# GpSimd makes the f32 normalised rows of tiles 1 to 3, and the sum of V's squares stands four products sooner in TensorE's list

## The chip, the cores and the metric

The kernel runs on one core of a Trainium2 chip. The metric is the device time of one execution in microseconds (us), the median of several runs. The engines are named as the profile names them: PE is TensorE's matmul unit, DVE is VectorE, ACT is ScalarE, POOL is GpSimd, SP is SyncE, whose queue issues most DMAs.

## The reference

Two gated blocks follow each other on x, which is 2 batches of 1024 rows of 2048 numbers in f32:

```
q(v, s, z) = (clip(round(v / s + z), 0, 255) - z) * s
x1 = x  + tanh(g_xattn) * ( q(layernorm(x)) @ q(ctx) )        # ctx: one 2048 x 2048 matrix per batch
y  = x1 + tanh(g_ffn)   * ( layernorm(x1) @ (U * S @ V.T).T ) # U, V: 2048 x 512, S: 512
```

The second product is computed in two steps with rank 512: h = layernorm(x1) @ V, then h @ (U * S).T.

## The kernel before

The 2048 rows are 16 tiles of 128 rows (8 per batch); a tile's row block is split in four column units of 512, and for some steps in two halves of 1024. Each engine has its own instruction list, written out by hand, and the engines meet through semaphores.

For a tile t the steps are these. `s1` is the quantised product on PE (64 matmuls, 16 for each column unit). POOL's `pre_row` and `pre` prepare the residual row in `ring`, with one multiplication over the row and four additions of the column correction. DVE's `x1_unit` adds the product to it (L1137) and takes its statistics (L1139). `stats2` makes mean and scale of the second layernorm (L1150 to L1162). Then the normalised row is written as a high and a low f16 part: ACT writes the high part of a half (`x_hi_half`, L811), DVE writes the normalised half in f32 into `xn` (L1174) and then the low part as the difference of `xn` and the high part (L1177); both lines stand in `x_lo_half`. `xn` is one buffer of one half, 128x1024. SP transposes the half by DMA into `xT` (L339), and PE's `mm3` multiplies it with the high and low parts of V, 24 matmuls for each half (L584, L589). `mm4` is the product with U (L650, L651, L655).

V and U are scaled by a power of two taken from their norms. ACT squares V in eight pieces (L859); PE sums these squares across the partitions with a product with ones (`norm_sums(0)`, L668); DVE's `norm_sum_up(0)` and `norm(0)` make the scale of it. Then ACT writes V's high parts (L877) and DVE its low parts (`v_low`, L1246) in eight pieces, between the low parts of tiles 0 and 1. PE's first product with V (tile 0, `mm3(0)`) takes the low parts in the order in which they are made. U follows in the same way (`u_low`, L1252).

On DVE the order around the change is: the last three `x1_unit` of tiles 0 to 2 with `norm(0)` between them, `x_lo` of tile 0, one unit of tile 3, `v_low` 0 and 1 with the statistics of tile 1 between, `v_low` 2 and 3, `x_lo_half(1, 0)`, `v_low` 4 to 7, `x_lo_half(1, 1)`, the statistics of tile 2, `norm(1)`, `hid_lo(0)`, `u_low(0)`, `x_lo` of tile 2, `u_low` 1 and 2, one unit of the output, `u_low(3)`. `x_lo` of tile 3 comes some 15 us later.

Of the kernel before, what the change touches and what calls it, by code (L numbers as in the profile page):

```python
# [7 lines left out]
def gated_block_program(nc, x, ctx_in, params, U_t, S, V, out):  # L8
    f32, bf16, f16 = mybir.dt.float32, mybir.dt.bfloat16, mybir.dt.float16
    i32, u8 = mybir.dt.int32, mybir.dt.uint8  # L10
    ALU, ACT, AX = mybir.AluOpType, mybir.ActivationFunctionType, mybir.AxisListType
# [8 lines left out]
    NQ = D // W  # L20
# [6 lines left out]
    G = 3  # L27
# [2 lines left out]
    GW = P // CG  # L30
    H_PE = (5, 6, 7)
    X_PE = TB - 1
    NU8 = 8
    EPS = 1e-5
    MAGIC = 1.5 * 2.0 ** 23
# [11 lines left out]
    with es:  # L47
# [3 lines left out]
        def sem(name):  # L51
            return es.enter_context(nc.semaphore(name))
# [8 lines left out]
        xn = sb("xn", [P, HW], f32)  # L61
# [3 lines left out]
        stage = sb("stage", [P, 2, CK, W], f32)  # L65
        u8r = sb("u8r", [P, NU8, CK * W], u8)
        ident_b = sb("ident_b", [P, P], bf16)
# [8 lines left out]
        ln2 = sb("ln2", [P, 2, 10], f32)  # L76
# [77 lines left out]
        ln2_ready = sem("ln2_ready")  # L154
# [8 lines left out]
        x1_ready = sem("x1_ready")  # L163
        st2_ready = sem("st2_ready")
        xn_ready = sem("xn_ready")
        xs_hi = sem("xs_hi")
        xs_lo = sem("xs_lo")
        mm3_half = sem("mm3_half")
# [26 lines left out]
        h_bank = lambda u: bank[3 + u % 2]  # L195
        x_dma = lambda u: u + 1 - (u > X_PE)
        x_bank = lambda g, half: bank[(2 * g + half) % 3]
# [12 lines left out]
        xhalf = lambda t, g: ring[:, t % R, (1 - g) * HW:(2 - g) * HW]  # L210
# [26 lines left out]
        @block.gpsimd  # L237
        def _(pool):
            def op2(c):
                b, n, i = chunk(c)  # L240
                if c in POOL_WHOLE:
                    pool.wait_ge(SPOT[c][1], LANDED[c])
                    nc.gpsimd.tensor_scalar(u8r[:, c % NU8, :], flat2(SPOT[c][0]), C_R2, P_Z2, ALU.mult, ALU.add)\  # L243
                        .then_inc(ctx_u8_pool, 1)
                    pool.wait_ge(ctx_u8_pool, POOL_WHOLE.index(c) + 1)
                else:
                    pool.wait_ge(ctx_u8, act_u8(c))
                if c == 0:
                    pool.wait_ge(centre_ready, 1)
                if b > 0:  # L250
                    pool.wait_ge(s1_done, unit(TB * b - 1, n) + 1)
                nc.gpsimd.tensor_scalar(q2_chunk(c), u8r[:, c % NU8, :], C_NC2, 1.0, ALU.add, ALU.mult)\  # L252
                    .then_inc(q2_pool, 1)

            def pre_row(t):
                pool.wait_ge(q_u8, part_count(t))
                pool.wait_ge(row_ready, t + 1)
                nc.gpsimd.tensor_scalar(xt(t), xt(t), bvec[:, t % R, 1:2], 1.0, ALU.add, ALU.mult).then_inc(x1_row, 1)  # L258

            def pre(t, n):  # L260
                pool.wait_ge(x1_row, t + 1)
                pool.wait_ge(corr_ready, NQ * (t // TB) + n + 1)
                nc.gpsimd.tensor_tensor(xq(t, n), xq(t, n), corr[:, n * W:(n + 1) * W], ALU.add).then_inc(x1_pre, 1)  # L263

            nc.gpsimd.memset(ident_b[:, :], 0.0).then_inc(setup_ready, 1)
            nc.gpsimd.memset(ones_f[:, :], 1.0).then_inc(setup_ready, 1)
            nc.gpsimd.memset(ones_b[:, :], 1.0).then_inc(setup_ready, 1)
            nc.gpsimd.memset(C_EPS, EPS).then_inc(setup_ready, 1)
            pool.wait_ge(setup_ready, 4)
            nc.gpsimd.affine_select(out=ident_b[:, :], in_=ident_b[:, :], compare_op=ALU.not_equal, fill=1.0,  # L270
                                    base=0, pattern=[[-1, P]], channel_multiplier=1).then_inc(ident_ready, 1)
            nc.gpsimd.memset(ones_h[:, :], 4.0 / GW).then_inc(setup_ready, 1)

            for c in range(CQ):
                if not on_dve(c):
                    op2(c)
            for n in range(NQ - 1):
                for i, c in enumerate(range(CQ * (n + 1), CQ * (n + 2), 2)):
                    op2(c)
                    if n == 0 and i < G:  # L280
                        pre_row(i)
                for t in range(G):
                    pre(t, n)
            for t in range(G):
                pre(t, NQ - 1)
            for t in range(G, NT):
                if t == TB:
                    for c in range(CB, 2 * CB):
                        op2(c)
                if t == G:  # L290
                    pool.wait_ge(t_written, 2 * G)
                    nc.gpsimd.memset(ident_h, 0.0).then_inc(ident_free, 1)
                    pool.wait_ge(ident_free, 1)
                    nc.gpsimd.affine_select(out=ident_h, in_=ident_h, compare_op=ALU.not_equal, fill=1.0, base=0,
                                            pattern=[[-1, P]], channel_multiplier=1).then_inc(ident_ready, 1)
                if t not in (6, 7):
                    pre_row(t)
                    for n in range(NQ):
                        pre(t, n)
                elif t == 6:  # L300
                    for v, n in MIXED:
                        if n == 0:
                            pre_row(v)
                        pre(v, n)
# [181 lines left out]
        def _(pe):  # L486
# [46 lines left out]
            def s1_part(t, n, k0=0, k1=KT):  # L533
                i = unit(t, n)
                if k0 == 0:
                    if t < G:
                        if n == 0:
                            pe.wait_ge(t_read, 2 * t + 1)
                        if n >= 2:
                            pe.wait_ge(x1_ready, unit(t, n - 2) + 1)  # L540
                    else:
                        if n == 0:
                            pe.wait_ge(qT_in, 16 * (t - G + 1))
                        if i < NQ * G + 3:
                            pe.wait_ge(x1_ready, unit(i - NQ * G, 2) + 1)
                        else:
                            pe.wait_ge(x1_ready, i - 2)
                        if t == TB and n == 0:
                            pe.wait_ge(corr_ready, 2 * NQ - 1)
                for k in range(k0, k1):  # L550
                    if t < G and n == 0 and k == KT // 2:
                        pe.wait_ge(t_read, 2 * t + 2)
                    mm = nc.tensor.matmul(unit_bank(t, n)[:, :], qT_of(t)[:, k, :], q2[:, n, k, :],  # L553
                                          start=(k == 0), stop=(k == KT - 1))
                if k1 == KT:
                    mm.then_inc(s1_done, 1)
# [5 lines left out]
            def mm3(u):  # L562
# [12 lines left out]
                for g in range(2):  # L575
                    if u == X_PE:
                        pe.wait_ge(xT_copied, 2 * g + 2)
# [15 lines left out]
            def x_pieces(g):  # L593
                pe.wait_ge(xs_hi, 2 * X_PE + g + 1)
                pe.wait_ge(xs_lo, 2 * X_PE + g + 1)
                for half in range(2):
# [99 lines left out]
                    for t in range(G if n < NQ - 1 else 1):  # L696
                        s1_part(t, n, CK * i, CK * i + CK)
            s1_part(1, NQ - 1)
            s1_part(2, NQ - 1, 0, 12)
            norm_sums(0)  # L700
            s1_part(2, NQ - 1, 12)
            s1(G)
            mm3(0)
            norm_sums(1)
# [43 lines left out]
        def _(act):  # L748
            def op1(c):
                act.wait_ge(SPOT[c][1], LANDED[c])  # L750
                if c >= NU8 and c < CB or c >= CB + NU8:
                    if on_dve(c - NU8):
                        act.wait_ge(q2_dve, dve_count(c - NU8))
# [50 lines left out]
            def x_hi_half(u, g):  # L804
                scale, bias = ln2[:, u % 2, 8:9], ln2[:, u % 2, 9:10]
                act.wait_ge(ln2_ready, u + 1)
                if u - 1 == X_PE:
                    act.wait_ge(xT_written, 2 * g + 2)
# [228 lines left out]
        def _(dve):  # L1037
            ts, stt, tt = nc.vector.tensor_scalar, nc.vector.scalar_tensor_tensor, nc.vector.tensor_tensor
# [129 lines left out]
            def x_lo_half(u, g):  # L1168
                mean, scale = ln2[:, u % 2, 0:1], ln2[:, u % 2, 8:9]
                if 2 * u + g > 0:  # L1170
                    dve.wait_ge(xs_lo, 2 * u + g)
                if u == 6 and g == 0:
                    dve.wait_ge(ctx_u8, act_u8(XN_CHUNK))
                ts(xn[:, :], xhalf(u, g), mean, scale, ALU.subtract, ALU.mult).then_inc(xn_ready, 1)  # L1174
                dve.wait_ge(xn_ready, 2 * u + g + 1)
                dve.wait_ge(xs_hi, 2 * u + g + 1)
                tt(xs[:, g, 1, :], xn[:, :], xs[:, g, 0, :], ALU.subtract).then_inc(xs_lo, 1)  # L1177

# [4 lines left out]
            def xT_copy(g):  # L1183
                for half in range(2):
                    dve.wait_ge(xT_written, 2 * g + half + 1)
                    dve.wait_ge(mm3_half, 2 * (X_PE - 1) + g + 1)
                    nc.vector.tensor_copy(xT[:, g, half, :, :].rearrange("p k w -> p (k w)"),
# [280 lines left out]
```

## Time and profile before

| | |
|---|---|
| median of 3 runs | 604.24 us (603.97 to 604.48) |
| the profiled execution | 604.71 us, its span 602.9 us |
| PE busy | 582.7 us, 97% of the span |
| DVE busy | 381.7 us, 63% |
| ACT busy | 212.4 us, 35% |
| POOL busy | 191.4 us, 32% |
| granted clock of TensorE | 1.000 |

All times of an event are microseconds from the start of the span. PE's matmuls overlap each other in the records: one of 512 columns is shown with 0.38 us, and begins 0.216 us behind the one before it. The name in front of the arrow is the tile that an instruction writes, those behind it are what it reads; `bank` is PSUM, the others are SBUF. The low part of V reads V from the space that is later `u_hl`, and so stands as `v_hl<-u_hl,wsc,v_hl`.

### The profile page before, as it was taken

To read this page: it belongs to the slowest core of one execution; us is meant where nothing else is said; L and a number is where in the kernel's file an instruction comes from. 1 tells how busy PE (TensorE), PEld (TensorE's weight loads), DVE (VectorE), ACT (ScalarE), POOL (GpSimd) and SP (SyncE) were. 2 spreads that over 40 slices of the span, in tenths; PEclk is the share of its full clock that TensorE was granted. 3 is DMA by queue.
4 is the path that set the end of the run, shared out by engine and by line. 5 is a ranking of instruction groups with operands and counts; after the bars stand their busy time and mean duration, and the time that the engine had idled before them with its cause. 6 is when DMAs were issued, how large, how long until landed. Compare 5 with 4: busy or idle time off the path is not lost.

```text
span 602.9 us, 7571 instructions
## 1 busy us (share of the span) xinstructions
PE 582.7 (97%) x2816; PEld 266.4 (44%) x2816; DVE 381.7 (63%) x703; ACT 212.4 (35%) x258; POOL 191.4 (32%) x149
## 2 busy tenths in 40 slices
PE   1899999999999999999999999999999999999998
PEld 1344444444444444445444444444444444444444
DVE  6939989995288962845375975647365665735212
ACT  5798978822041432456623310303011030301000
POOL 2899650002223419726505800220404030030000
DMA  8999985639828795998835344370906345181512
GB/s 280 387 387 387 309 240 128 116 122 196 239 55 240 186 216 189 241 304 268 241 123 150 81 84 54 66 190 12 223 35 147 116 90 172 30 163 20 138 53 104
DMA packets 143828, 102.21 MB, mean 170 GB/s; under 512 B 106672, under 2 KB 106928, under 8 KB 143792
## 3 DMA queue, kind: packets, MB, share of 16 engines
q1 hardware_dynamic: 134800, 84.43, 53.1%
q10 hardware_dynamic: 8992, 17.30, 9.2%
q8 instruction: 22, 0.36, 0.2%
q14 instruction: 14, 0.11, 0.1%
HBM read 58.99 MB, written 16.78 MB: 126 GB/s over the span
## 4 chain that ended last, share of the span: by engine, by line
PE 75%; DMA 11%; DVE 8%; issue 3%; SPq 2%; ACT 1%; POOL 1%; DVEq 0%; ACTq 0%
PE bank L553 23%; PE bank L584 16%; PE bank L651 8%; PE bank L650 8%; PE bank L655 8%; PE bank L589 8%; DMA v_hl<-in_ctx_dram 8%; DMA xT<-xs 4%; DVE v_hl L1246 1%; DVE xn L1174 1%; DVE xs L1177 1%; DVE ring L1137 1%; SPq L311 1%; PE bank L520 1%; POOL u8r L243 1%
## 5 line engine op out<-in xcount | busy, mean ns | idle before, releaser
L553 PE MATMUL bank<-q,qT 128*128 128x512 bf16 x896 | 201.5, 380 | 0.3 <-DVE ring L1137 0.3
L553 PEld LDWEIGHTS bank<-q,qT 128*128 128x128 bf16 x896 | 87.7, 98 | 107.1 <-issue 1.5
L258 POOL TENSOR_SCALAR ring<-ring,bvec 128x2048 f32<-128x2048 f32 x16 | 32.8, 2050 | 269.7 <-DVE bvec L1119 269.7
L584 PE MATMUL bank<-v_hl,xT 128*128 128x512 f16 x512 | 115.8, 379 | 0.9 <-DMA xT<-xs 0.9
L263 POOL TENSOR_TENSOR ring<-ring,corr 128x512 f32<-128x512 f32 x64 | 87.0, 1390 | 23.2 <-ACT corr L850 22.1
L651 PE MATMUL bank<-u_hl,hbuf 128*128 128x512 f16 x240 | 91.1, 380 | 0.0
L650 PE MATMUL bank<-u_hl,hbuf 128*128 128x512 f16 x240 | 91.0, 379 | 0.0
L1137 DVE SCALAR_TENSOR_TENSOR ring<-bank,const,ring 128x512 f32<-128x512 f32 x64 | 47.6, 743 | 58.2 <-PE bank L553 55.9
L1210 DVE SCALAR_TENSOR_TENSOR ring<-bank,cy,ring 128x512 f32<-128x512 f32 x63 | 46.4, 747 | 52.8 <-PE bank L655 52.8
L252 POOL TENSOR_SCALAR q<-u8r,const 128x1024 bf16<-128x1024 uint8 x52 | 63.9, 1236 | 45.4 <-ACT u8r L756 41.7
L584 PEld LDWEIGHTS bank<-v_hl,xT 128*128 128x128 f16 x512 | 49.8, 98 | 61.2 <-DMA xT<-xs 1.9
L797 ACT ACTIVATE ln<-ln,const 128x1 f32<-128x1 f32 x16 | 4.7, 294 | 189.8 <-DVE ln L1150 189.8
L655 PE MATMUL bank<-u_hl,hbuf 128*128 128x512 f16 x240 | 61.6, 379 | 0.0
L589 PE MATMUL bank<-v_hl,xT 128*128 128x512 f16 x256 | 60.6, 379 | 0.0
L1177 DVE TENSOR_TENSOR xs<-xn,xs 128x1024 f16<-128x1024 f32 x32 | 46.8, 1461 | 9.7 <-ACT xs L811 8.8
L1078 DVE BATCH_NORM_STATS2 st<-ring 128x6 f32<-128x512 f32 x64 | 40.3, 680 | 10.3 <-DMA ring<-in_x_dram 10.2
L1139 DVE BATCH_NORM_STATS2 st<-ring 128x6 f32<-128x512 f32 x64 | 44.5, 695 | 2.2
L811 ACT ACTIVATE xs<-ring,ln 128x1024 f16<-128x1024 f32 x32 | 38.2, 1233 | 20.4 <-DVE ln L1162 14.8
L589 PEld LDWEIGHTS bank<-v_hl,xT 128*128 128x128 f16 x256 | 25.0, 98 | 30.4 <-DVE v_hl L1246 0.4
L650 PEld LDWEIGHTS bank<-u_hl,hbuf 128*128 128x128 f16 x240 | 23.5, 98 | 28.5 <-issue 0.4
L655 PEld LDWEIGHTS bank<-u_hl,hbuf 128*128 128x128 f16 x240 | 23.5, 98 | 28.3
L1193 DVE SCALAR_TENSOR_TENSOR hbuf<-bank,hbuf 128x512 f16<-128x512 f32 x16 | 11.0, 687 | 39.4 <-ACT hbuf L825 39.4
(136 smaller groups left out, 493.3 us busy)
## 6 DMA issues: line engine op xcount, KB each, us to landing
out_dram<-ring SPq DMA_DIRECT2D x63, 256.0 KB, 3.5
ring<-in_x_dram SPq DMA_DIRECT2D x62, 256.0 KB, 3.9
v_hl<-in_ctx_dram SPq DMA_DIRECT2D x26, 512.0 KB, 11.5
stage<-in_ctx_dram ACTq DMA_DIRECT2D x17, 512.0 KB, 5.8
u_hl<-in_L_ffn_V_dram SPq DMA_DIRECT2D x8, 512.0 KB, 11.5
corr<-in_ctx_dram ACTq DMA_DIRECT2D x8, 512.0 KB, 6.7
stage<-in_ctx_dram SPq DMA_DIRECT2D x6, 512.0 KB, 11.5
q<-in_ctx_dram ACTq DMA_DIRECT2D x4, 512.0 KB, 8.8
```

What stands on the lines that cost most here:

```text
L252: nc.gpsimd.tensor_scalar(q2_chunk(c), u8r[:, c % NU8, :], C_NC2, 1.0, ALU.add, ALU.mult)\
L263: nc.gpsimd.tensor_tensor(xq(t, n), xq(t, n), corr[:, n * W:(n + 1) * W], ALU.add).then_inc(x1_pre, 1)
L553: mm = nc.tensor.matmul(unit_bank(t, n)[:, :], qT_of(t)[:, k, :], q2[:, n, k, :], start=(k == 0), stop=(k == KT - 1))
L584: nc.tensor.matmul(h_bank(u)[:, :], xT[:, g, half, k % 8, :], v_hl[:, k, 0, :], start=(g == 0 and a == 0 and half == 0), stop=False)
L589: mm = nc.tensor.matmul(h_bank(u)[:, :], xT[:, g, 0, k % 8, :], v_hl[:, k, 1, :], start=False, stop=(g == 1 and a == 7))
L650: nc.tensor.matmul(y_bank(i)[:, :], t_hi[:, r, :], u_hl[:, n, r, 0, :], start=(r == 0), stop=False)
L651: nc.tensor.matmul(y_bank(i)[:, :], t_lo[:, r, :], u_hl[:, n, r, 0, :], start=False, stop=False)
L655: mm = nc.tensor.matmul(y_bank(i)[:, :], t_hi[:, r, :], u_hl[:, n, r, 1, :], start=False, stop=(r == RT - 1))
L1137: stt(xq(t, n), unit_bank(t, n)[:, :], C_A, xq(t, n), ALU.mult, ALU.add).then_inc(x1_ready, 1)
L1139: nc.vector.bn_stats(st2[:, t % R, n, :], xq(t, n)).then_inc(st2_ready, 1)
L1177: tt(xs[:, g, 1, :], xn[:, :], xs[:, g, 0, :], ALU.subtract).then_inc(xs_lo, 1)
L1210: stt(xq(u, n), y_bank(i)[:, :], cy[:, n:n + 1], xq(u, n), ALU.mult, ALU.add).then_inc(y_ready, 1)
```

## The change

POOL gets six new instructions behind the four additions of tile 3: for tiles 1, 2 and 3 and both halves it writes `xn`. Each waits for the tile's mean and scale (`ln2_ready`) and for the difference before it (`xs_lo`), since `xn` is one buffer. DVE leaves out its own six and waits for POOL's (`xn_pool`). Besides, PE's `norm_sums(0)` moves from behind the twelfth to behind the eighth of the sixteen products of tile 2's last unit.

```diff
+    XN_POOL = (1, 2, 3)
...
+        xn_pool = sem("xn_pool")
...
+            def normalised_x(u, g):
+                mean, scale = ln2[:, u % 2, 0:1], ln2[:, u % 2, 8:9]
+                pool.wait_ge(ln2_ready, u + 1)
+                pool.wait_ge(xs_lo, 2 * u + g)
+                nc.gpsimd.tensor_scalar(xn[:, :], xhalf(u, g), mean, scale, ALU.subtract, ALU.mult).then_inc(xn_pool, 1)
...
                     pre_row(t)
                     for n in range(NQ):
                         pre(t, n)
+                    if t == G:
+                        for u in XN_POOL:
+                            for g in range(2):
+                                normalised_x(u, g)
...
             s1_part(1, NQ - 1)
-            s1_part(2, NQ - 1, 0, 12)
+            s1_part(2, NQ - 1, 0, 8)
             norm_sums(0)
-            s1_part(2, NQ - 1, 12)
+            s1_part(2, NQ - 1, 8)
...
-                ts(xn[:, :], xhalf(u, g), mean, scale, ALU.subtract, ALU.mult).then_inc(xn_ready, 1)
-                dve.wait_ge(xn_ready, 2 * u + g + 1)
+                if u in XN_POOL:
+                    dve.wait_ge(xn_pool, 2 * XN_POOL.index(u) + g + 1)
+                else:
+                    ts(xn[:, :], xhalf(u, g), mean, scale, ALU.subtract, ALU.mult).then_inc(xn_ready, 1)
+                    dve.wait_ge(xn_ready, 2 * (u - sum(v < u for v in XN_POOL)) + g + 1)
                 dve.wait_ge(xs_hi, 2 * u + g + 1)
                 tt(xs[:, g, 1, :], xn[:, :], xs[:, g, 0, :], ALU.subtract).then_inc(xs_lo, 1)
```

The lists of the engines, first POOL's, before, from the identity matrix to tile 5's additions:

```order
L292 MEMSET ident_b 128x128
L294 AFFINE_SELECT ident_b<-ident_b 128x128
L258 TENSOR_SCALAR ring<-ring,bvec 128x2048
L263 TENSOR_TENSOR ring<-ring,corr 128x512 x4
L258 TENSOR_SCALAR ring<-ring,bvec 128x2048
L263 TENSOR_TENSOR ring<-ring,corr 128x512 x4
```

and POOL's of the change, at the same place:

```order
L300 MEMSET ident_b 128x128
L302 AFFINE_SELECT ident_b<-ident_b 128x128
L260 TENSOR_SCALAR ring<-ring,bvec 128x2048
L271 TENSOR_TENSOR ring<-ring,corr 128x512 x4
L266 TENSOR_SCALAR xn<-ring,ln 128x1024 x6
L260 TENSOR_SCALAR ring<-ring,bvec 128x2048
```

The six new instructions stand between tile 3's additions and tile 4's row.

DVE's list before, from the last scale of tile 1 to its second difference and the first statistics of tile 2 (`v_hl<-` is a low part of V):

```order
L1162 TENSOR_SCALAR ln<-ln 128x1
L1246 SCALAR_TENSOR_TENSOR v_hl<-u_hl,wsc,v_hl 128x2x512 x2
L1174 TENSOR_SCALAR xn<-ring,ln 128x1024
L1177 TENSOR_TENSOR xs<-xn,xs 128x1024
L1246 SCALAR_TENSOR_TENSOR v_hl<-u_hl,wsc,v_hl 128x2x512 x4
L1174 TENSOR_SCALAR xn<-ring,ln 128x1024
L1177 TENSOR_TENSOR xs<-xn,xs 128x1024
L1150 BN_AGGR ln<-st 128x2
```

and DVE's of the change:

```order
L1174 TENSOR_SCALAR ln<-ln 128x1
L1261 SCALAR_TENSOR_TENSOR v_hl<-u_hl,wsc,v_hl 128x2x512 x2
L1192 TENSOR_TENSOR xs<-xn,xs 128x1024
L1261 SCALAR_TENSOR_TENSOR v_hl<-u_hl,wsc,v_hl 128x2x512 x4
L1192 TENSOR_TENSOR xs<-xn,xs 128x1024
L1162 BN_AGGR ln<-st 128x2
```

The differences are left (now L1192), and the two that made `xn` are gone from between the low parts of V.

PE's list before, around the sum of V's squares (`bank<-ssq,ones_f`):

```order
L516 MATMUL bank<-q,ones_b 128x512 x2
L553 MATMUL bank<-q,qT 128x512 x2
L553 MATMUL bank<-q,xT 128x512 x28
L668 MATMUL bank<-ssq,ones_f 128x8
L553 MATMUL bank<-q,xT 128x512 x4
L553 MATMUL bank<-q,qT 128x512 x64
```

and PE's of the change:

```order
L528 MATMUL bank<-q,ones_b 128x512 x2
L565 MATMUL bank<-q,qT 128x512 x2
L565 MATMUL bank<-q,xT 128x512 x24
L680 MATMUL bank<-ssq,ones_f 128x8
L565 MATMUL bank<-q,xT 128x512 x8
L565 MATMUL bank<-q,qT 128x512 x64
```

Four of the products that stood ahead of the sum now stand behind it.

## Rows read from the trace of the kernel before

**Rows 1.** The page's first part: busy us, share of the span, instructions.

```profile
PE 582.7 (97%) x2816; PEld 266.4 (44%) x2816; DVE 381.7 (63%) x703; ACT 212.4 (35%) x258; POOL 191.4 (32%) x149
```

**Rows 2.** PE's waits: us in total, times, longest.

```profile
PE bank L516 <- POOL q L252: 13.6, 4, 11.3
...
PE bank L584 <- DMA xT<-xs: 0.9, 2, 0.5
```

**Rows 3.** PE's timeline, 76 to 109 us: start, us, instruction, [idle before, releaser].

```profile
76.95 0.28 PE L668 MATMUL bank<-ssq,ones_f 128*128 128x8 f32 x2
...
100.40 1.99 PE L589 MATMUL bank<-v_hl,xT 128*128 128x512 f16 x8
102.22 0.29 PE L668 MATMUL bank<-ssq,ones_f 128*128 128x8 f32 x2
...
105.81 1.89 PE L589 MATMUL bank<-v_hl,xT 128*128 128x512 f16 x8
108.12 3.63 PE L584 MATMUL bank<-v_hl,xT 128*128 128x512 f16 x16 [0.41 <-DMA xT<-xs]
```

**Rows 4.** The chain that ended last, 98 to 108 us: start, us, what.

```profile
98.05 3.67 DVE v_hl L1246 x3
...
102.49 1.24 DVE xs L1177
...
103.80 4.27 DMA xT<-xs
```

**Rows 5.** DVE's timeline, 77 to 103 us.

```profile
77.28 0.17 DVE L1223 TENSOR_REDUCE wsc<-bank 128x1 f32<-128x8 f32 x1 [1.22 <-PE bank L668]
...
82.27 0.85 DVE L1174 TENSOR_SCALAR xn<-ring,ln 128x1024 f32<-128x1024 f32 x1
83.15 2.18 DVE L1177 TENSOR_TENSOR xs<-xn,xs 128x1024 f16<-128x1024 f32 x1
...
92.49 2.47 DVE L1246 SCALAR_TENSOR_TENSOR v_hl<-u_hl,wsc,v_hl 128x1024 f16<-128x1024 f32 x2
94.88 0.81 DVE L1174 TENSOR_SCALAR xn<-ring,ln 128x1024 f32<-128x1024 f32 x1
95.72 1.23 DVE L1177 TENSOR_TENSOR xs<-xn,xs 128x1024 f16<-128x1024 f32 x1
96.86 4.87 DVE L1246 SCALAR_TENSOR_TENSOR v_hl<-u_hl,wsc,v_hl 128x1024 f16<-128x1024 f32 x4
```

**Rows 6.** ACT's timeline, the last square of V.

```profile
74.08 0.19 ACT L859 ACTIVATION_READ_ACCUMULATOR hbuf<-u_hl 128x1 f32 x1
```

**Rows 7.** Timelines of POOL and of DVE where both work.

```profile
81.28 2.96 POOL L263 TENSOR_TENSOR ring<-ring,corr 128x512 f32<-128x512 f32 x2
...
207.01 2.11 POOL L263 TENSOR_TENSOR ring<-ring,corr 128x512 f32<-128x512 f32 x1
...
208.03 1.64 DVE L1174 TENSOR_SCALAR xn<-ring,ln 128x1024 f32<-128x1024 f32 x1
209.71 2.17 DVE L1177 TENSOR_TENSOR xs<-xn,xs 128x1024 f16<-128x1024 f32 x1
```

**Rows 8.** Single lines: ns min/median/max, first and last start, forms.

```profile
L1177 DVE TENSOR_TENSOR xs<-xn,xs x32: 1224/1226/2873, 83.2 to 554.9; 128x1024 f16<-128x1024 f32 x32
...
L1137 DVE SCALAR_TENSOR_TENSOR ring<-bank,const,ring x64: 730/745/753, 44.6 to 548.2; 128x512 f32<-128x512 f32 x64
...
L258 POOL TENSOR_SCALAR ring<-ring,bvec x16: 1965/1972/2399, 32.4 to 526.4; 128x2048 f32<-128x2048 f32 x16
...
L243 POOL TENSOR_SCALAR u8r<-v_hl,const,par x5: 1188/1190/1618, 13.6 to 23.9; 128x1024 uint8<-128x1024 f32 x5
...
L263 POOL TENSOR_TENSOR ring<-ring,corr x64: 1259/1268/2249, 43.3 to 532.1; 128x512 f32<-128x512 f32 x64
```

**Rows 9.** Timelines of DVE and of PE, tile 2 and the last low parts of U.

```profile
113.36 1.23 DVE L1177 TENSOR_TENSOR xs<-xn,xs 128x1024 f16<-128x1024 f32 x1
...
120.47 2.73 DVE L1252 SCALAR_TENSOR_TENSOR u_hl<-u8r,us_scale,u_hl 128x512 f16<-128x512 f32 x4
...
122.80 1.03 PE L655 MATMUL bank<-u_hl,hbuf 128*128 128x512 f16 x4
```

## The prediction

> **What bounds the kernel now.** The page's first part comes first: TensorE (PE) is busy for 582.7 of the 602.9 us of the span [rows 1]. The view of PE's waits then says what the rest is: 13.6 us behind POOL's quantised chunks, in the opening stage, and of the small ones the one that lies at this change is for a DMA of xs into xT, 0.9 us in two waits [rows 2]. So a change around tiles 1 to 3 can only give back what PE loses there, and everything else it does matters only if it makes PE wait anew.
>
> What PE loses there is read from its timeline. A product with 512 columns is shown with 0.38 us, and 16 of them with 3.63 [rows 3], so each follows the one before in (3.63 - 0.38) / 15, about 0.216 us. The second half of tile 1's product with V should follow eight products that begin at 105.81, that is at 105.81 + 8 x 0.216 = 107.54; it begins at 108.12 [rows 3]: 0.58 us lost. Eight products from 100.40 should hand over at 102.13, and the next begins at 102.22: 0.09 lost. The sum is 0.67 us, and this is the most that the change can save here.
>
> The chain that ended last says who is late at both places [rows 4]. VectorE (DVE) ends the last low part of V at 101.73 (98.05 + 3.67), then makes xn, then the difference xs until 103.72; the transposing DMA of tile 1's second half lands 4.27 us after 103.80, and PE starts. So DVE's list from 77 to 104 us is the term to be costed. In it the reader should see one thing: DVE is busy without a gap from 77.28 to 103.72, with xn (0.81 us each), the differences (1.23 us) and the eight low parts (2.47 us for two, 4.87 for four) [rows 5].
>
> **Part 1, the sum of squares four products sooner.** The last square ends at 74.27 (74.08 + 0.19) [rows 6]; the sum would now stand at 76.95 - 4 x 0.216 = 76.09, still 1.8 us behind it, so PE has nothing to wait for. PE's own work is the same. DVE, which took this sum at 77.28, takes it at 76.42: 0.86 us earlier. How far does this get? xn of tile 0 began at 82.27 [rows 5] and would begin at 81.41. But POOL is adding the correction to row 3: one addition starts at 81.28 and two of them last 2.96 us, until 84.24 [rows 7]. Group 7 also shows what happens when these two engines meet: at 208.03 xn takes 1.64 us instead of 0.81, and at 209.71 the difference takes 2.17 instead of 1.23, beside an addition that takes 2.11 us instead of 1.27 [rows 7, 8]. They take turns: each instruction waits for the other engine's to end. In the profile shown the difference at 83.15 took 2.18 us [rows 5], so it ended 1.1 us behind POOL's additions, which is nearly its own whole length. With xn at 81.41, POOL's third addition is already in (it began 0.13 us before), xn ends near 83.1 as now, the fourth addition comes next, and the difference still ends at 85.33. The 0.86 us end there. I cost part 1 at nothing; if DVE were to come in ahead, that is a rival below.
>
> **Part 2, POOL makes xn of tiles 1 to 3.** Removed from DVE: six instructions of 0.81 us, with 0.03 us to the next start: 0.84 each (94.88 to 95.72) [rows 5]. Added on POOL: six tensor_scalar of 128x1024 in f32, which no row shows. From below: half of POOL's 128x2048 one, 1.97 / 2 = 0.99 us; from above, of this kind, the one of 128x1024 that writes uint8, 1.19 us [rows 8]. I take 1.1, between them. POOL's timeline is empty from 84.24 until row 4's correction, behind tile 3's differences, so nothing of POOL's list is queued behind the new waits that anyone needs; it issues no DMA here either.
>
> What the cover costs is DVE's. For tile 1 POOL can begin when the scale is ready, near 92.6, and DVE is then in two low parts of V that began at 92.49, with four more from 96.86 in front of the second half [rows 5]. Such a low part reads two tensors in SBUF (V in f32 and its high part). No row shows this instruction beside a working POOL. The nearest rows are the differences, which also read two tensors in SBUF and are stretched (1.22 us at least, up to 2.87), while L1137, which reads one from PSUM and one from SBUF, never goes above 0.753 us in 64 [rows 8]. I therefore take it that the low parts take turns with POOL as the differences do. The stretch is 2.17 - 1.23 = 0.94 us behind an addition of 1.27 us, and 0.94 - (1.27 - 1.10) = 0.77 behind one of 1.1 us. I take 0.85, between these. The bounds are 0 (no turns at all) and 1.27 (one whole addition).
>
> The Trainium skill (SBUF — State Buffer, Who interferes with whom) says that a VectorE instruction with two SBUF inputs contends with a GpSimd instruction that reads SBUF, and that whichever issues first holds the shared ports for its whole length while the other fully blocks. The differences' rows agree with it, and it speaks against this change: by it the work moved to POOL still takes VectorE's time at the low parts.
>
> The sum for tile 1. First half: DVE saves 0.84 and loses 0.85 at the low part behind POOL. Second half: POOL's instruction falls among the four low parts, and these are late by the first half's 0.01 plus 0.85. The last low part ends at 101.73 + 0.86 = 102.59. PE needs it for the last two of its eight products from 100.40, and had it just in time; so PE is now 0.86 us late and would reach tile 1's second half at 107.54 + 0.86 = 108.40. The second difference gets its own 0.84 back and ends at 103.74, against 103.72; the DMA lands near 108.1, before PE is there. The stall of 0.58 us is gone and a new one of 0.86 + the old 0.09 has taken its place, one stage earlier: PE goes on at 108.40 instead of 108.12, **0.28 us later**.
>
> Tile 2: its two differences follow each other on DVE, and xn is a single buffer, so the second xn can only start behind the first difference. DVE saves 0.84 once and then stands for POOL's 1.1 us and two semaphores instead of its own 0.84: about 0.5 us saved at best, and the first difference has to wait for ScalarE's half anyway. The two end near 114.6, as now (113.36 + 1.23) [rows 9]. What is behind them is the low parts of U, the last of which run from 120.47 to 123.20, while PE takes the first of them at 122.80 and one every 0.22 us, the fourth at 123.45 [rows 9]: 0.25 us to spare, 0.5 with PE 0.28 late. I cost it at nothing; without the cover it costs what DVE is later by. Tile 3 saves DVE about 0.5 us too, where it waits for PE soon after: nothing.
>
> After 125 us the rows of PE's waits name only fractions of a microsecond, and DVE, ACT and the DMA queues follow PE's progress, so 0.28 us is carried to the end. Against the profiled execution, 604.71 (span 602.9 and 1.8 around it), this makes 605.0; its own time lies 0.47 above the median of the runs, 604.24, and on that median it makes **604.5**.
>
> **Rivals.** (a) The low parts don't take turns with POOL. For it: no row shows them together. Against: the differences do. Then the last low part ends at 100.0, the difference near 102.1, and PE has neither stall: 604.24 - 0.67 = 603.6. Chance 0.14.
> (b) The 0.86 us of part 1 get through, because DVE comes in before POOL's third addition. For it: only 0.13 us decide. Against: the fourth addition still has to be passed. Then the last low part is where it was, 101.73, the DMA lands at 107.2 and PE runs on at 107.54: 603.7. Chance 0.10.
> (c) The slower side: POOL's new instruction holds the turn longer. The mechanism is the one of the sum, its price is PE's lateness of 2h - 0.84 - 0.58, with h the stretch of one low part. It passes 1.2 us from h = 1.31. For it: POOL's additions cost 1.27 us for 512 columns, and at that rate 1024 columns would be 2.5 us, with h near 2.2 and PE 3.0 us late: 607.2. Against: its tensor_scalar rows, with one tensor read, run at under 1 ns a column. At the upper bound of h, 1.27, it makes 604.24 + 1.12 = 605.4. Chance of more than 1.2 us: 0.08.
> (d) The low parts, issued back to back, keep POOL out until the list has a gap. Then DVE stands for POOL's 1.1 us at each half: the second difference ends about 0.7 later and so does the DMA, near 108.8: 604.9. It has the forecast's sign and is counted with it.
>
> **The numbers.** The forecast with (d) has 0.62, with a range of its own of 604.3 to 604.9. The rivals (a) to (c) have 0.14, 0.10 and 0.08, and 0.06 is for what I have not seen, such as a transfer that falls elsewhere. The range goes from (a) less the spread of the runs (0.2) to (c) at its upper bound plus the same: 603.4 to 605.6. A measurement of this kernel tells about 0.2%, 1.2 us, from no change. Faster than 603.0 needs (a) and part of another stall too: 0.05. Slower than 605.4: (c) and a share of the unseen, 0.10. Within: 0.85.
>
> **What the changed profile would show.** Right: the low parts of V beside POOL's xn last about 2.1 us instead of 1.3, one in each half of tile 1; PE stops for about 0.9 us before 102 to 103 us, behind the low part of V, and no longer behind the DMA of xs; the first difference of tile 0 still ends near 85.3. Wrong: low parts that keep 1.3 us with POOL working (a), tile 0's difference near 84.5 (b), POOL's xn above 1.3 us (c), POOL starting only when the low parts are through (d), or a PE wait beyond 125 us that is new and longer than half a microsecond.

## The result and the profile after

The change makes the kernel slower: 612.94 us median of 4 runs (612.34 to 613.82) against 604.36 of before beside it, a ratio of 1.0143 (95% interval 1.013 to 1.0156). The forecast was 604.5 with a range of 603.4 to 605.6. The profiled execution has a span of 610.5 us, 7.6 more than before.

The page's first part of the changed kernel, which answers to [rows 1] (some matmul records are missing):

```profile
PE 585.1 (96%) x2787; PEld 267.1 (44%) x2816; DVE 379.7 (62%) x697; ACT 212.4 (35%) x258; POOL 218.0 (36%) x155
```

DVE has lost six instructions, but POOL has gained 26.6 us for six. The view of one line says why; it is POOL's new instruction, ns min/median/max:

```profile
L266 POOL TENSOR_SCALAR xn<-ring,ln x6: 3782/3784/5854, 92.3 to 141.8; 128x1024 f32<-128x1024 f32 x6
```

It takes **3.78 us** where nothing disturbs it. The prediction had 1.1, between 0.99 and 1.19. Its timeline, POOL, 90 to 146 us:

```profile
92.34 5.85 POOL L266 TENSOR_SCALAR xn<-ring,ln 128x1024 f32<-128x1024 f32 x1 [8.43 <-DVE ln L1174]
99.68 5.71 POOL L266 TENSOR_SCALAR xn<-ring,ln 128x1024 f32<-128x1024 f32 x1 [1.49 <-DVE xs L1192]
...
115.77 3.78 POOL L266 TENSOR_SCALAR xn<-ring,ln 128x1024 f32<-128x1024 f32 x1 [3.61 <-DVE xs L1192]
```

And DVE's timeline at the same place, which answers to [rows 5]:

```profile
92.14 2.47 DVE L1261 SCALAR_TENSOR_TENSOR v_hl<-u_hl,wsc,v_hl 128x1024 f16<-128x1024 f32 x2
98.28 1.22 DVE L1192 TENSOR_TENSOR xs<-xn,xs 128x1024 f16<-128x1024 f32 x1 [3.67 <-POOL xn L266]
99.42 5.65 DVE L1261 SCALAR_TENSOR_TENSOR v_hl<-u_hl,wsc,v_hl 128x1024 f16<-128x1024 f32 x4
...
119.64 1.23 DVE L1192 TENSOR_TENSOR xs<-xn,xs 128x1024 f16<-128x1024 f32 x1 [4.05 <-POOL xn L266]
```

The two low parts from 92.14 keep their length (2.47), and it is POOL that waits: 5.85 us is 3.78 and 2.07 more. Then DVE stands for 3.67 us. From 92.14 to the end of the last low part at 105.07 it takes 12.93 us, against 9.24 before (92.49 to 101.73). In front of the second half it is one of the four low parts that is held up as well, the third, with 2.05 us instead of 1.28:

```profile
101.83 2.05 DVE L1261 SCALAR_TENSOR_TENSOR v_hl<-u_hl,wsc,v_hl 128x1024 f16<-128x1024 f32 x1
```

PE's timeline pays for it, beside [rows 3]:

```profile
100.76 0.61 PE L601 MATMUL bank<-v_hl,xT 128*128 128x512 f16 x2 [0.40 <-DVE v_hl L1261]
101.96 0.60 PE L601 MATMUL bank<-v_hl,xT 128*128 128x512 f16 x2 [0.60 <-DVE v_hl L1261]
103.94 0.60 PE L601 MATMUL bank<-v_hl,xT 128*128 128x512 f16 x2 [1.37 <-DVE v_hl L1261]
105.13 1.03 PE L601 MATMUL bank<-v_hl,xT 128*128 128x512 f16 x2 [0.59 <-DVE v_hl L1261]
...
106.25 6.14 PE L596 MATMUL bank<-v_hl,xT 128*128 128x512 f16 x16
```

Each pair of products stands for its low part of V, 3.0 us in all. The sixteen products from 106.25 take 6.14 us instead of 3.6: the windows view has a mean granted clock of 0.56 from 105.90 to 112.20, so PE ran there mostly at 1.2 of its 2.4 GHz (columns: us, busy by engine, clock, DMA share, GB/s):

```profile
105.90:112.20 6.30, 6.30 (x19) 2.48 (x18) 5.85 (x22) 2.53 (x6) 3.78 (x1) 0.56 0.44 85
```

From 105.13 to the products at 112.22 PE takes 7.09 us; the same work takes 4.04 in experiment 5 (106.01 to 110.05), where the granted clock is 1.0. PE begins the product with U at 119.13 instead of 113.31, and 3.05 of these 5.82 us are the slower clock. A second loss comes at tile 5, where PE waits for qT, the tile's transposed quantised row. From PE's timeline:

```profile
187.44 13.76 PE L565 MATMUL bank<-q,qT 128*128 128x512 bf16 x62 [1.88 <-DMA qT<-qn]
```

This product began at 178.92 before, without a wait: PE is 8.5 us late here. The chain that ended last leads from the slow instruction at tile 3, through DVE and the output's DMAs, to tile 5's transposition (us from start, us, what):

```profile
136.54 3.79 POOL xn L266
...
145.68 1.23 DVE xs L1192
...
182.91 4.26 DMA qT<-qn
```

Behind it some small waits of before are gone, such as the one for xs that ended at 268.99, and the span ends 7.6 us later.

### The profile page after: what moved, and what is told of

It is laid out like the page before. It is cut to its first block, busy times and chain, and to the rows that moved or that the text cites. A ratio compares the mean times of both kernels' runs of the same rounds, so it can differ in the third digit from the quotient of the medians.

```text
span 610.5 us, 7548 instructions
## 1 busy us (share of the span) xinstructions
PE 585.1 (96%) x2787; PEld 267.1 (44%) x2816; DVE 379.7 (62%) x697; ACT 212.4 (35%) x258; POOL 218.0 (36%) x155
## 4 chain that ended last, share of the span: by engine, by line
PE 66%; DVE 10%; DMA 9%; POOL 6%; issue 3%; ACT 3%; SPq 2%; ACTq 0%; DVEq 0%; POOLq 0%
PE bank L565 22%; PE bank L596 14%; PE bank L662 7%; PE bank L667 7%; PE bank L663 7%; PE bank L601 7%; POOL xn L266 3%; DMA stage<-in_ctx_dram 2%; DVE xs L1192 2%; DMA u_hl<-in_L_ffn_V_dram 2%; DMA v_hl<-in_ctx_dram 2%; DMA out_dram<-ring 2%; POOL ring L271 1%; DVE u_hl L1267 1%; DVE ring L1149 1%
## 5 line engine op out<-in xcount | busy, mean ns | idle before, releaser
L565 PE MATMUL bank<-q,qT 128*128 128x512 bf16 x873 | 198.6, 380 | 3.5 <-DMA qT<-qn 1.9
L596 PE MATMUL bank<-v_hl,xT 128*128 128x512 f16 x512 | 118.2, 385 | 0.0
L601 PE MATMUL bank<-v_hl,xT 128*128 128x512 f16 x256 | 61.4, 381 | 3.0 <-DVE v_hl L1261 3.0
L1192 DVE TENSOR_TENSOR xs<-xn,xs 128x1024 f16<-128x1024 f32 x32 | 46.8, 1461 | 23.1 <-POOL xn L266 14.4
L266 POOL TENSOR_SCALAR xn<-ring,ln 128x1024 f32<-128x1024 f32 x6 | 26.7, 4450 | 35.0 <-DVE ln L1174 28.4
```

The costliest lines, as they stand in the source:

```text
L266: nc.gpsimd.tensor_scalar(xn[:, :], xhalf(u, g), mean, scale, ALU.subtract, ALU.mult).then_inc(xn_pool, 1)
L596: nc.tensor.matmul(h_bank(u)[:, :], xT[:, g, half, k % 8, :], v_hl[:, k, 0, :], start=(g == 0 and a == 0 and half == 0), stop=False)
L601: mm = nc.tensor.matmul(h_bank(u)[:, :], xT[:, g, 0, k % 8, :], v_hl[:, k, 1, :], start=False, stop=(g == 1 and a == 7))
```

## The experiments

Intervals are those of the ratio to the kernel before, run on the same chip.

**1. The same change with another operation.** ALU.add with -mean, which `ln2` holds already, in place of ALU.subtract with the mean.

```diff
-                mean, scale = ln2[:, u % 2, 0:1], ln2[:, u % 2, 8:9]
+                neg, scale = ln2[:, u % 2, 2:3], ln2[:, u % 2, 8:9]
-... xhalf(u, g), mean, scale, ALU.subtract, ALU.mult)
+... xhalf(u, g), neg, scale, ALU.add, ALU.mult)
```

Expected: 

> The changed kernel with one operation replaced: GpSimd makes xn as (x + neg) * scale, with neg = -mean, which VectorE has written already, instead of (x - mean) * scale. Theory (the subtraction is what makes GpSimd's instruction take 3.78 us): it takes 1.0 to 1.2 us; the low parts of V wait little, TensorE's four waits before 106 us shrink to under 1 us, its clock stays at 1.0, and the time is 604.0 to 605.2 us. Rival (two column scalars with an f32 output are slow whatever the operation): the instruction stays at 3.8 us and the time at 612 to 614 us.

Measured: 605.15 us, ratio 1.0014 (1.0006 to 1.0023). The line of the new instruction, DVE's stretched low part and PE's waits in this kernel:

```profile
L266 POOL TENSOR_SCALAR xn<-ring,ln x6: 1195/1196/3273, 92.7 to 133.9; 128x1024 f32<-128x1024 f32 x6
```

```profile
99.56 2.05 DVE L1261 SCALAR_TENSOR_TENSOR v_hl<-u_hl,wsc,v_hl 128x1024 f16<-128x1024 f32 x1
```

```profile
PE bank L565 <- DMA qT<-qn: 1.0, 1, 1.0
PE bank L601 <- DVE v_hl L1261: 0.8, 2, 0.6
```

One operation takes 3.78 us down to 1.20 and about nine tenths of the loss away. The 1.0 us at qT is a single wait before 180.80, at tile 5, where the kernel before had none.

**2. Which forms are slow.** Eight instructions at an idle end of POOL's list, in the kernel before.

```diff
+            for s1_, s2_, o1, o2 in forms:
+                pool.wait_ge(probe, done)
...
+                    ins = nc.gpsimd.tensor_scalar(pb, pa, s1_, s2_, o1, o2)
+                ins.then_inc(probe, 1)
```

Expected: 

> The kernel before, with two fills and eight GpSimd tensor_scalar instructions of 128x1024, f32 to f32, in an idle end of GpSimd's list behind tile 15's last difference, each waiting for the one before; they compute nothing that is used. In order: (subtract, mult), (add, mult), (mult, add), all three with two columns; (subtract, mult) and (add, mult) with a column and the constant 1.0; (mult, subtract) with two columns; subtract alone; add alone. Theory (subtraction is slow): 3.8 us for the forms with subtract, 1.0 to 1.2 us for those with add and mult. Rival (two columns are slow): the first, second, third and sixth take 3.8 us, the others near 1.1. The kernel's time is that of before, since nothing waits for them.

Measured: POOL's timeline, in the order of the list:

```profile
556.78 3.79 POOL L325 TENSOR_SCALAR stage<-stage,pc 128x1024 f32<-128x1024 f32 x1
560.67 1.19 POOL L325 TENSOR_SCALAR stage<-stage,pc 128x1024 f32<-128x1024 f32 x1
561.96 1.19 POOL L325 TENSOR_SCALAR stage<-stage,pc 128x1024 f32<-128x1024 f32 x1
563.25 3.70 POOL L325 TENSOR_SCALAR stage<-stage,pc 128x1024 f32<-128x1024 f32 x1
567.05 1.11 POOL L325 TENSOR_SCALAR stage<-stage,pc 128x1024 f32<-128x1024 f32 x1
568.27 3.78 POOL L325 TENSOR_SCALAR stage<-stage,pc 128x1024 f32<-128x1024 f32 x1
572.14 2.86 POOL L323 TENSOR_SCALAR stage<-stage,pc 128x1024 f32<-128x1024 f32 x1
575.09 2.85 POOL L323 TENSOR_SCALAR stage<-stage,pc 128x1024 f32<-128x1024 f32 x1
```

Every pair with subtract takes 3.70 to 3.79 us, (add, mult) and (mult, add) 1.11 to 1.19, with two columns or one. Each form ran once. The rival falls, and so does one part of the theory: subtract alone takes 2.86 us where 3.8 were expected, and add alone takes 2.85, as long. So it is the pair (add, mult) or (mult, add) that is fast, not the addition. Why the pairs differ, no run shows. The kernel took 604.25 us.

**3. The sum's new place alone.** Expected: 

> The kernel before with only the sum of V's squares moved four products ahead; VectorE makes every xn. Theory (the turn-taking with GpSimd's additions at 81 to 84 us eats what VectorE gains): tile 0's first difference ends within 0.4 us of where it did, 85.3, and the time is that of before within 0.5 us. Rival (the gain gets through to the last low part of V): up to 0.7 us less than before.

The edit is the last part of the change without the rest. Measured: 604.37 us, ratio 1.0003 (0.9995 to 1.0012). DVE's timeline in this kernel:

```profile
81.43 1.70 DVE L1174 TENSOR_SCALAR xn<-ring,ln 128x1024 f32<-128x1024 f32 x1
83.17 2.18 DVE L1177 TENSOR_TENSOR xs<-xn,xs 128x1024 f16<-128x1024 f32 x1
```

xn begins 0.84 us sooner than in [rows 5] and takes 0.85 longer. Nothing gets through.

**4. GpSimd's part alone.** The change with `norm_sums(0)` behind the twelfth product. Expected: 

> The changed kernel with the sum of V's squares at its old place; GpSimd makes xn of tiles 1 to 3 with the subtraction. Theory (all of the loss is the six instructions of 3.78 us): 612 to 614 us, as the whole change. Rival (the sum's new place has a share of the loss): below 611 us.

Measured: 614.72 us, ratio 1.0173 (1.0157 to 1.0189). The whole loss and 0.3% more, a little above the 612 to 614 us expected. In this execution POOL's second instruction took 6.90 us instead of 5.71: it was let in one low part later, so one run of the turns costs a low part more than the other. That this is all of the 0.3% isn't shown.

**5 and 6. Which tile.** XN_POOL = (1,) and XN_POOL = (2, 3), both with the subtraction. Expected of the first: 

> The changed kernel with GpSimd making xn of tile 1 only, still with the subtraction; VectorE makes that of tiles 2 and 3. Theory (the loss is made at tile 1, where the low parts of V wait in line behind the first difference): TensorE starts the first product with U about 5.8 us later than before, as in the whole change, and the time is 610 to 613.5 us. Rival (tiles 2 and 3 make most of it): under 608 us.

Of the second: 

> The changed kernel with GpSimd making xn of tiles 2 and 3 only, with the subtraction. VectorE's second difference of tile 2 then ends about 3 us later than before (3.8 us of GpSimd in place of 0.84 of its own), and behind it the low parts of U had 0.25 us to spare. Theory (each tile's pair has its own cover, tile 2's is 0.25 us): TensorE waits 2 to 3 us for the low parts of U, 606 to 608 us. Rival (tile 2's differences have slack): that of before within 0.6 us.

Measured: 609.32 us, ratio 1.0078 (1.0065 to 1.0092), and 609.63 us, ratio 1.0081 (1.0067 to 1.0095). Both lie outside what was expected: tile 1 costs less than the 610 to 613.5 us that I wrote (PE begins the product with U 5.06 us later, at 118.37, not 5.8), tiles 2 and 3 cost more than 606 to 608. The two losses add up to 1.6%, the whole change has 1.4. PE's waits with tiles 2 and 3 only:

```profile
PE bank L565 <- DMA qT<-qn: 2.1, 1, 2.1
PE bank L667 <- DVE u_hl L1267: 1.6, 4, 0.8
```

The low parts of U are the cover of 0.25 us that the prediction had named [rows 9]. The other wait it had not: tile 3's differences end later, behind them on DVE stand the quantisation and the row of tile 4, and the transposed tile 4 reaches PE 2.1 us late. A third part is the clock again, which fell behind the four short stops at the low parts of U (same columns as above):

```profile
120.00:123.50 3.50, 3.25 (x8) 1.24 (x9) 3.50 (x7) 3.04 (x5) 0.00 (x0) 0.54 0.42 78
```

PE took 3.64 us from 120.25 to 123.89 for nine products, which at 0.216 us each is 1.94: 1.7 us lost.

**7. The gap filled.** Products in front of PE's four waits, in the changed kernel:

```diff
+                            for _ in range((2, 3, 6, 3)[a // 2]):
+                                nc.tensor.matmul(bank[5][:, :], xT[:, g, 0, k % 8, :], v_hl[:, k, 0, :],
+                                                 start=True, stop=True)
```

Expected: 

> The changed kernel with 14 products of 512 columns more in TensorE's list, before the four waits for the last low parts of V, into a PSUM bank that is free there; their result is not used. They take about the 3.0 us in which TensorE stood. Theory (the stops before 105 us made the granted clock fall to 1.2 GHz for 6.8 us behind them, and this cost about 2.5 us more): the granted clock stays at 1.0 from 31 us on, TensorE reaches the first product with U 2 to 2.7 us sooner, and the time is 1.5 to 3 us under that of the whole change of this chip. Rival (the clock's fall has another cause or is made up for later): the same time as the whole change, 612 to 614 us, or more by the extra products.

Measured: 615.47 us, ratio 1.018 (1.0165 to 1.0195). In the profile the clock stayed at 1.0 (two of the other three executions have means of 0.994 and 0.997) and the product with U began at 118.38, 0.75 us sooner than in the changed kernel, but no time was saved. Three waits took it: xs of tile 1 (1.3 us, PE was there ahead of the DMA), the low parts of U (1.6), and this one:

```profile
PE bank L565 <- DMA qT<-qn: 3.1, 1, 3.1
```

This is a miss: 1.5 to 3 us less than the whole change were expected, and the time is 2.5 us more. DVE and POOL were later than in the changed kernel here (POOL's second instruction again took 6.90 us), so the two times don't compare cleanly. What can be said: PE had DVE's list to wait for behind the slow stretch in any case. That the stops make the clock fall isn't shown either: in the profile with tile 1 only, PE stood 3.2 us in the same four places and its clock stayed at 1.0. Nor is it shown that the fall lengthens the whole kernel: the four executions of the changed kernel had mean clocks of 0.994, 0.997, 0.997 and 1.000 and took 612.34, 612.40, 613.82 and 613.48 us, so the one without a fall is not the shortest. With tile 1 only, the one at 1.000 is the longest of four (609.94 us; the others, at 0.996 and 0.997, took 608.87 to 609.47).

**8 and 9. Room for VectorE instead.** In the kernel before, POOL's last two additions of tile 3, which aren't needed until 123 us, wait for tile 1's differences; 8 has the sum's new place too, 9 hasn't.

```diff
                     for n in range(NQ):
+                        if t == G and n == 2:
+                            pool.wait_ge(xs_lo, 4)
                         pre(t, n)
```

Expected of 8: 

> The kernel before with the sum of V's squares four products ahead and with GpSimd's last two additions of tile 3 held back until tile 1's differences are done (a wait for the fourth low part of x); VectorE makes every xn. Theory (VectorE loses 0.95 us to these additions at tile 0, and the sum's 0.86 us end there): tile 0's first xn and difference take 0.81 and 1.23 us, the last low part of V ends about 1.8 us sooner, near 99.9, TensorE's two stalls before 108.2 us (0.09 and 0.58) are gone, and the time is 0.4 to 0.9 us less than before. Rival (something else holds VectorE there or a later wait takes it back): that of before within 0.3 us.

Of 9: 

> The kernel before with GpSimd's last two additions of tile 3 held back until tile 1's differences are done; the sum of V's squares at its old place. Theory (VectorE loses about 0.95 us at tile 0 to these additions, and that alone already covers TensorE's two stalls): the last low part of V ends near 100.8, tile 1's second difference near 102.8, its DMA lands near 107.2 before TensorE is there, and the time is 0.3 to 0.9 us under before. Rival (only both together save anything): before within 0.3 us.

Of 8 once more: 

> The version with the sum of V's squares ahead and the two additions of tile 3 held back, once more, on this chip and beside the version without the sum. Theory: 0.4 to 0.9 us under before, as the first time (0.6), and not more than 0.3 us from the version without the sum, since each of the two edits alone makes the room that TensorE's stalls need. Rival (the first comparison was the spread of the runs): the interval holds 1.0.

Measured: 8 is 603.74 us, ratio 0.9989 (0.998 to 0.9998), and again 603.55, ratio 0.9984 (0.9976 to 0.9993); 9 is 603.89, ratio 0.9998 (0.9989 to 1.0007). DVE's timeline of 8:

```profile
81.12 0.80 DVE L1176 TENSOR_SCALAR xn<-ring,ln 128x1024 f32<-128x1024 f32 x1
81.95 1.23 DVE L1179 TENSOR_TENSOR xs<-xn,xs 128x1024 f16<-128x1024 f32 x1
```

Both at their own length, and in 8 and 9 alike PE's waits between 72 and 150 us are gone. The interval of 9 doesn't tell it from no change nor from 8. Version 8 is about 0.6 us under the kernel before in both comparisons, with intervals below 1, close to the 0.67 us that PE lost here. In its profile the last low part of V ends at 99.58 (expected near 99.9), in that of 9 at 100.44 (expected near 100.8).

**10 and 11. The fast form, by tiles.** Experiment 1 with XN_POOL = (2, 3), and with (1,). Expected of 10: 

> The changed kernel with the addition of -mean in place of the subtraction, and GpSimd making xn of tiles 2 and 3 only. Theory (at 1.20 us for one instruction only tile 1, where the low parts of V meet it, costs anything): that of before within 0.4 us. Rival (tile 2's second difference is late by enough to hold up the low parts of U): 0.5 to 1.5 us over before.

Of 11: 

> The same, with GpSimd making xn of tile 1 only. Theory: the two low parts of V in front keep GpSimd out, VectorE stands for about 1.1 us at the first difference, and the second GpSimd instruction stretches one low part by 0.8: TensorE waits about 0.8 us and gets 0.6 back at the DMA; 0.2 to 1.0 us over before. Rival (the whole of the 1.0 us by which this form was over before with all three tiles comes from tiles 2 and 3): before within 0.2 us.

Measured: 604.77 us, ratio 1.0009 (1.0001 to 1.0018), and 605.01, ratio 1.0012 (1.0002 to 1.0021). PE's timeline of 11:

```profile
102.72 0.61 PE L601 MATMUL bank<-v_hl,xT 128*128 128x512 f16 x2 [0.99 <-DVE v_hl L1261]
```

PE waits 0.99 us for tile 1's low part where 0.8 was expected. The time, 0.85 us over the kernel before by the medians, lies in the 0.2 to 1.0 that were. Tiles 2 and 3 were expected within 0.4 us of no change and are 0.6 over by the medians (0.1 to 1.1 by the interval), so the rival, 0.5 to 1.5, fits as well. The profile of 10 doesn't show it: its span, 602.6 us, is no longer than before, and behind 107.94 no wait of PE longer than 0.3 us stands in it. Where the excess would come from stays open.

## Why the prediction was wrong

**The step that failed** is the duration in part 2: "From below: half of POOL's 128x2048 one, 1.97 / 2 = 0.99 us; from above, of this kind, the one of 128x1024 that writes uint8, 1.19 us [rows 8]. I take 1.1". It is 3.78. The two rows [rows 8] are an (add, mult) and a (mult, add); the new instruction is a (subtract, mult). The bound "from above" was one of shape alone, and the operations were taken to cost the same. Rival (c) had the right suspicion, a GpSimd instruction too long for its place, and was dismissed with the same rows: "its tensor_scalar rows, with one tensor read, run at under 1 ns a column". Its 2.5 us, taken from the additions, would have been short as well. Its way of charging the length is wrong too: it stretches both low parts by h, and with 3.78 us h would be 0.94 - (1.27 - 3.78) = 3.45, which makes 604.24 + 2 x 3.45 - 0.84 - 0.58 = 609.7. The runs show h at 0.77 as before. The length comes in by another door, DVE's wait for xn at the first half (3.67 us), and as PE's wait at tile 5's transposition (1.88), which the prediction put at nothing.

With that term near its forecast (experiment 1, 1.20 us) the time, 605.15, lies inside the stated range, but the forecast's 0.3 us over the kernel before are 0.8 to 1.0 (the medians: 604.14 to 604.36 before). At the product with U PE is 0.50 us late (113.81 against 113.31) where 0.28 was the forecast. The rest comes at a wait of 0.97 us at 180.80, for tile 5's transposition, less the wait of 0.51 at 268.99 that is gone. The rest of the working, point by point:

- *Part 1 costs nothing.* Right, and for the reason given (experiment 3): the fourth addition has to be passed, and the difference ends at 85.35, as before. Rival (b) is out.
- *The low parts of V take turns with GpSimd.* Right in that they hold each other up: one among the four low parts in front of the second half takes 2.05 us, 0.77 more than 1.28, in the changed kernel and in experiment 1. Rival (a) is out. But "each instruction waits for the other engine's to end" is not what happened: in the changed kernel it lost 0.77 us beside an instruction of 3.78, and the low part after it kept 1.27 us. The working took the stretch to grow with GpSimd's length, 0.87 us for 1.20; that its lower value is 0.77 is luck.
- *One stretch in each half.* Wrong. In the first half it went as in (d): two low parts issued back to back kept POOL out for 2.07 us, in every kernel with POOL at tile 1. In the second half POOL came in at the third or at the fourth. So the first half costs DVE the whole wait for POOL, 1.08 us in experiment 1 and 3.67 in the change.
- *PE gets 0.58 back at the DMA.* The stall for tile 1's second half was gone, as said, and the new one stood at the low parts of V. It was not gone in experiment 5, where POOL came in one low part later: PE waited 1.24 us there.
- *Tile 2 and tile 3 cost nothing.* This rested on POOL's 1.1 us. At 3.78 and without tile 1, the cover of 0.25 us at the low parts of U was gone, and tile 3's differences, which were said to be "where it waits for PE soon after", pushed tile 4's transposition past PE's need; in the whole change, where PE is late already, it is tile 5's. Tiles 2 and 3 alone cost 0.8%. At 1.20 us it is not quite nothing either: the 0.97 us at 180.80 are what the prediction named as a sign of being wrong, a new wait beyond 125 us of more than half a microsecond. With tile 1 alone (experiment 11) PE waits 0.47 us at 155.73 for tile 4's transposition, with tiles 2 and 3 alone (10) for none, so tile 1's lateness has a part in it; the shares stay open.
- *Nothing of the clock was in the forecast.* In the changed kernel it fell for about 6 us and cost 3.05 us there. What it cost in the end can't be told from these runs, since DVE is late behind it in any case.
- *Two slips in the working.* Rival (a) has the last low part end at 100.0; it is 101.73 - 0.84 = 100.89, which its 102.1 for the difference goes with, and its time stays. And the chances 0.05, 0.85 and 0.10 are cut at 603.0 and 605.4, not at the ends of the range, 603.4 and 605.6.

## What to carry to other kernels

Before work is moved to another engine, find a row of the same operations on that engine, not only of the same shape: on GpSimd the pair of operations alone made a factor of three, and (x - m) * s can be written as (x + (-m)) * s. An engine that stands idle is not free cover when the instructions beside it on VectorE read two tensors in SBUF: here GpSimd waited 2.07 us for two of them and one of them lost 0.77 to it. And a single buffer between two engines puts the whole duration of the slower one into the list of the other. Where VectorE was the late one here, GpSimd work taken out of its way saved 0.6 us, while work given to GpSimd cost 0.8 us even in the fast form.

## What the runs showed of the hardware

- GpSimd's tensor_scalar, 128x1024 in f32: 1.11 to 1.20 us as (add, mult) or (mult, add), 3.70 to 3.79 as (subtract, mult) or (mult, subtract), 2.85 to 2.86 with one operation, add or subtract.
- A low part of V is stretched by 0.77 us beside GpSimd's instruction, whether that one takes 1.20 or 3.78 us. The Trainium skill (SBUF — State Buffer, SBUF: two separate sides) has whichever of the two starts first hold the shared port pair for its whole instruction, with the other fully blocked. The additions' rows look like that, the slow form's don't: here the low part lost 0.77 of 3.78 us, and the measurement decides.
- VectorE's low parts, issued without a gap, kept GpSimd out for two instructions (2.07 us) each time at the first half, and for two or three at the second. Who gets the next turn differs between executions of nearly the same program, and one turn is worth 1.2 us to GpSimd.
- The granted clock fell behind four stops of PE, 3.0 us in all, in the changed kernel (0.50 from 105.13 to 106.25, 0.56 from 105.90 to 112.20), and behind four stops of 1.6 us in all in experiment 6 (0.54 from 120.00 to 123.50). It stayed at the upper level behind four stops of 3.2 us in the profile of experiment 5. At the lower level one product of 512 columns followed the other in 0.43 us (120.64 and 121.07 in experiment 6), at the upper in 0.216.
